# Expert stages of a two-layer macaron block: gate and up weights fetched per block into four fixed buffers and used as the stationary operand

## The chip, the cores and the metric

The kernel runs on one core of one Trainium2 chip. The metric is the device time of one execution in microseconds (us); the median of the runs is what counts.

## The reference

Four batches of 512 rows of 256 features pass through seven steps. Only the two that use `_L1_ffn_ref` are touched:

```python
    x = x + 0.5 * _L0_ffn_ref(_layernorm(x), ...)
    x = x + _L0_attn_ref(_layernorm(x), ...)
    x = x + 0.5 * _L0_ffn_ref(_layernorm(x), ...)
    x = x + 0.5 * _L1_ffn_ref(_layernorm(x), ...)     # stage m1
    x = x + _L1_attn_ref(_layernorm(x), ...)
    x = x + 0.5 * _L1_ffn_ref(_layernorm(x), ...)     # stage m2

    def _L1_ffn_ref(hidden_states, gate_weight, up_weight, down_weight, topk_idx, topk_weight):
        B, S, H, I, E, K = (4, 512, 256, 128, 32, 4)
        ...
        xs = x[tok_sorted]                    # rows ordered by expert, 4 experts per row
        g = jax.lax.ragged_dot(xs, jnp.swapaxes(gate_weight, 1, 2), group_sizes)
        u = jax.lax.ragged_dot(xs, jnp.swapaxes(up_weight, 1, 2), group_sizes)
        hmid = jax.nn.silu(g) * u
        o = jax.lax.ragged_dot(hmid, jnp.swapaxes(down_weight, 1, 2), group_sizes)
        o = o * flat_weight[perm][:, None]
        y = jnp.zeros((n, h), dtype=x.dtype).at[tok_sorted].add(o)
```

The experts are drawn anew from the inputs, so which expert a block of rows needs is known only at run time. All of it is in fp32.

## The kernel before, in words

**The whole.** `program` builds four stages that follow each other in each engine's stream: `first_layer` (the first three steps, and the routing of rows to experts), `moe_stage` with the tag m1, `latent_stage` (the second attention), `moe_stage` with the tag m2. There is no scheduler: each engine's program is written out by hand in a function of its own, and the order on an engine is the order in the code. Engines meet at semaphores (`wait_ge`, `then_inc`).

**Rows and blocks.** The 2,048 rows times 4 experts are laid out in DRAM (`rows_dram`) in blocks of 128 rows, a block having one expert. `NRUN` is 95 blocks, run in both expert stages. GpSimd scatters each normalised row to its place with an indirect DMA whose row numbers lie in `slot` (number = block times 128 plus place in the block). `block_expert` holds the expert of each block in SBUF.

**The arena.** `arena` is 96 KB per partition and, in an expert stage, holds the gate and up weights of all 32 experts (`GU`, 64 KB per partition, 512 columns per expert) and behind them the down weights (`DW`, 32 KB). In the attention stages the same bytes hold other things, so the weights are loaded in six parts of 2 MB: `early` (parts 4 and 5, which are DW), `middle` (0 and 2) and `late` (1 and 3) for m1, and three again during `latent_stage` (`reloads`: part 3, 5, 4).

**One block of an expert stage.** TensorE turns the block's rows (two transposes, L1267, into `psX`); ScalarE copies them to `xgT` (L1182); TensorE multiplies with the rows as the stationary operand and 256 columns of gate and up weights as the moving one, twice because 256 features are two partitions' worth (L1276, into `psG`, which then has rows on partitions); ScalarE takes the silu of the gate half (L1188, `sg`), VectorE multiplies it with the up half (L1214, `hm`); TensorE turns that (L1285, `psH`), VectorE copies it (L1221, `hT`), TensorE multiplies with the down weights (L1292, `psY`), ScalarE copies the result (L1194, `ys`, eight buffers), and GpSimd scatters it to `outs_dram` (the indirect DMA of L167). An fp32 product is two records in the trace, two passes over the moving operand; a transpose is one.

**The order on TensorE** is a software pipeline over blocks: in step b the transposes of block b+1, the load of block b's expert number into a register (`value_load`, L1270), the gate and up product of block b, the turn of `hm` of block b-1, the down product of block b-2. The expert number sets the address of the weights of L1276 and L1292.

**The order on SyncE's queue**: four 128 KB loads for the first four blocks, then one load of 512 KB per group of four blocks into one of two halves of `xg` (L1131), each waiting until a half is free (`turned`). Behind each of these stands, in m1, one of 16 loads of weights for the second attention (L1154) and in m2, at eight of them, a copy of a batch of `x` out to DRAM (L1146) or back in another order (L1151).

**The ends.** Before a stage TensorE waits for all weights (`experts_in`) and for the scattered rows (`placed`). After the last block, SyncE waits until all outputs have landed (`saved`), and the gathering of outputs begins.

## Time and profile before

| | us |
|---|---|
| median of 3 runs | 1455.6 (1455.46 to 1456.02) |
| profiled execution | 1455.02 |
| its span, first to last instruction | 1453.2 |
| m1, from the first transposes to the last blocks | 508 to 669 |
| m2, the same | 1256 to 1420 |
| TensorE matmuls busy | 1252.3, 86% of the span |
| VectorE, ScalarE, GpSimd busy | 950.3, 670.5, 490.6 |
| DMA moved | 151.87 MB, mean 105 GB/s |

The profile has a page and a trace. The page gives busy time per engine, the span in 40 slices, the chain of work that ended last, and the costliest groups of instructions. A group of TensorE has a busy time that counts overlapping records once and a mean duration of one record that includes the drain of the array, so records overlap and their mean times their count is more than the time they take. What a pass really takes in the stream is read from the chain of waits, or from a run of many. The trace answers for a stretch, a line, a tile or a queue.

### The profile page before, as it was taken

To read this page: it belongs to the slowest core of one execution; us is meant where nothing else is said; L and a number is where in the kernel's file an instruction comes from. 1 tells how busy PE (TensorE), PEld (TensorE's weight loads), DVE (VectorE), ACT (ScalarE), POOL (GpSimd) and SP (SyncE) were. 2 spreads that over 40 slices of the span, in tenths; PEclk is the share of its full clock that TensorE was granted. 3 is DMA by queue.
4 is the path that set the end of the run, shared out by engine and by line. 5 is a ranking of instruction groups with operands and counts; after the bars stand their busy time and mean duration, and the time that the engine had idled before them with its cause. 6 is when DMAs were issued, how large, how long until landed. Compare 5 with 4: busy or idle time off the path is not lost.

```text
span 1453.2 us, 22278 instructions
## 1 busy us (share of the span) xinstructions
PE 1252.3 (86%) x6593; PEld 818.3 (56%) x6594; DVE 950.3 (65%) x2794; ACT 670.5 (46%) x1700; POOL 490.6 (34%) x493
## 2 busy tenths in 40 slices
PE   6879888898888399998879799889889997699997
PEld 4554243343324388886645466546556655578886
DVE  6796758777778422224698878987988794133334
ACT  2205655556563055553345444554455453255550
POOL 3054040053123645552211211251143143455550
PEclk8989999999999699999998899999999999799999
DMA  8527543066313266544011000020000102355647
GB/s 288 110 31 122 183 73 58 1 120 187 135 40 146 98 232 202 193 158 170 15 44 30 20 10 1 12 105 1 2 35 24 59 30 94 127 193 179 210 140 304
DMA packets 79119, 151.87 MB, mean 105 GB/s; under 512 B 11677, under 2 KB 60254, under 8 KB 75422
## 3 DMA queue, kind: packets, MB, share of 16 engines
q1 hardware_dynamic: 63310, 108.59, 25.7%
q0 software_dynamic: 15264, 41.70, 8.0%
q8 instruction: 59, 0.97, 0.3%
q14 instruction: 54, 0.44, 0.1%
q10 hardware_dynamic: 432, 0.17, 0.0%
HBM read 85.29 MB, written 64.75 MB: 103 GB/s over the span
## 4 chain that ended last, share of the span: by engine, by line
PE 54%; DVE 28%; ACT 8%; issue 5%; DMA 3%; POOL 2%; SPq 0%; DVEq 0%; ACTq 0%; POOLq 0%
PE m_psG L1276 12%; PE m_psY L1292 6%; DVE a_t L1740 4%; DVE a_mx L924 4%; PE a_psA L1490 3%; DVE a_nb L1748 3%; PE a_psO L482 3%; ACT a_pr L1609 3%; PE m_psX L1267 3%; PE a_psU L1478 3%; PE a_psO L1514 2%; PE a_psU L457 2%; PE a_psU L1469 2%; PE a_psS L468 2%; PE a_psW L447 2%
## 5 line engine op out<-in xcount | busy, mean ns | idle before, releaser
L1609 ACT ACTIVATE a_pr<-a_psA,a_nb 128x512 f32<-128x512 f32 (+3 forms) x256 | 132.6, 524 | 229.9 <-DVE a_nb L1748 227.8
L167 POOL DMA_INDIRECT outs_dram<-m_ys,dest x190 | 182.2, 959 | 153.4 <-ACT m_ys L1194 148.2
L1214 DVE TENSOR_TENSOR m_hm<-m_psG,m_sg 128x128 f32<-128x128 f32 x190 | 55.3, 291 | 250.9 <-ACT m_sg L1188 249.8
L924 DVE TENSOR_REDUCE a_mx<-a_psU 128x1 f32<-128x512 f32 x256 | 163.3, 683 | 64.3 <-PE a_psU L457 63.1
L1276 PE MATMUL m_psG<-arena,m_xgT 128*128 x760 | 199.4, 385 | 3.6 <-ACT m_xgT L1182 3.5
L1664 POOL TENSOR_TENSOR a_q<-a_q,a_t 64x512 f32<-64x512 f32 x64 | 81.0, 1266 | 347.6 <-DVEq L1743 323.9
L167 POOL DMA_INDIRECT rows_dram<-a_xd,slot x112 | 114.1, 1019 | 157.1 <-DVE a_xd L147 72.8
L610 ACT ACTIVATE a_P<-a_psS 128x512 f32<-128x512 f32 x256 | 142.7, 597 | 51.2 <-PE a_psS L468 48.9
L1276 PEld LDWEIGHTS m_psG<-arena,m_xgT 128*128 128x128 f32 x760 | 129.5, 190 | 18.7 <-issue 7.5
L1748 DVE TENSOR_REDUCE a_nb<-a_psA 128x1 f32<-128x512 f32 (+3 forms) x256 | 113.2, 484 | 30.9 <-PE a_psA L1493 21.5
L457 PE MATMUL a_psU<-arena 96*128 96x512 bf16 x256 | 102.1, 399 | 26.2 <-DVE a_mx L924 24.8
L1292 PE MATMUL m_psY<-arena,m_hT 128*128 x380 | 113.6, 382 | 0.0
L468 PE MATMUL a_psS<-arena 108*128 108x512 bf16 x256 | 98.3, 389 | 9.6 <-ACT a_P L610 9.1
L1490 PE MATMUL a_psA<-arena,a_q 128*128 128x512 f32 (+3 forms) x256 | 91.9, 471 | 16.7 <-ACT a_pr L1609 16.0
L1758 DVE TENSOR_SCALAR a_pr<-a_pr,a_rec 128x512 f32<-128x512 f32 (+3 forms) x256 | 98.0, 404 | 6.8
L1182 ACT COPY m_xgT<-m_psX 128x256 f32<-128x256 f32 x190 | 71.8, 378 | 64.6 <-PE m_psX L1267 64.4
L1188 ACT ACTIVATE m_sg<-m_psG 128x128 f32<-128x128 f32 x190 | 52.7, 277 | 91.0 <-PE m_psG L1276 90.9
L1194 ACT COPY m_ys<-m_psY 128x256 f32<-128x256 f32 x190 | 70.7, 372 | 51.3 <-PE m_psY L1292 51.0
L1490 PE MATMUL a_psA<-a_kT,a_q 128*128 128x512 f32 (+3 forms) x256 | 87.8, 453 | 7.5 <-ACT a_pr L1609 7.3
L1598 ACT COPY a_prT<-a_psP 128x1280 f32<-128x1280 f32 x64 | 78.8, 1231 | 28.7 <-PE a_psP L1504 28.7
L1740 DVE TENSOR_TENSOR a_t<-a_psU,la_sin 32x512 f32<-32x512 f32 x128 | 87.9, 687 | 1.7
L1504 PE MATMUL a_psP<-ident,a_pr 128*128 128x128 f32 x640 | 81.8, 275 | 2.0 <-ACT a_prT L1598 2.0
(299 smaller groups left out, 2286.2 us busy)
## 6 DMA issues: line engine op xcount, KB each, us to landing
m_xg<-rows_dram SPq DMA_DIRECT2D x46, 512.0 KB, 4.2
arena<-in_mo_w SPq DMA_DIRECT2D x9, 2048.0 KB
arena<-part_dram SPq DMA_DIRECT2D x96, 128.0 KB, 5.9
arena<-outs_dram SPq DMA_DIRECT2D x20, 512.0 KB, 4.0
rows_dram<-a_P SPq DMA_DIRECT2D x6, 1024.0 KB, 11.6
part_dram<-a_part SPq DMA_DIRECT2D x16, 384.0 KB, 5.4
rows_dram<-arena SPq DMA_DIRECT2D x6, 1024.0 KB, 13.0
arena<-outs_dram SPq DMA_DIRECT2D x6, 1024.0 KB, 12.0
```

The costliest lines, as they stand in the source:

```text
L167: pool.indirect_dma_start(out=rows_dram, out_offset=bass.IndirectOffsetOnAxis(ap=slot[:, c:c + 1], axis=0), in_=row, in_offset=None).then_ ...
L457: pe.matmul(psU[n % 2][:, :], QS[0:NT, o + h * L + qt * P:o + h * L + (qt + 1) * P], KS[0:NT, o + h * L:o + (h + 1) * L], start=True, stop ...
L468: pe.matmul(psS[n % 2][:, :], KS[0:KC, o + h * L + kt * P:o + h * L + (kt + 1) * P], QS[0:KC, o + h * L:o + (h + 1) * L], start=True, stop ...
L610: act.activation(Pr[:, o:o + L], psS[c % 2][:, :], ACT.Exp).then_inc(exp_done, 1)
L924: dve.tensor_reduce(mx[g % 2][:, 4 * kt + qt:4 * kt + qt + 1], psU[n % 2][:, :], AX, ALU.max).then_inc(u_free, 1)
L1276: ins = pe.matmul(psG[b % 2][:, 0:2 * INTER], xgT[:, (b % 2) * D + k * P:(b % 2) * D + (k + 1) * P], GU[:, ds(e * (KD * 2 * INTER) + k * 2 ...
L1292: pe.matmul(psY[m % 2][:, 0:D], hT[:, (m % 2) * P:(m % 2 + 1) * P], DW[:, ds(e * D, D)], start=True, stop=True).then_inc(y_done, 1)
L1490: pe.matmul(psA[:, AT[t]:AT[t] + (t + 1) * P], qh[:, t * P:(t + 1) * P], kh[:, 0:(t + 1) * P], start=(t == BANKS[k][0]), stop=False, skip_ ...
L1609: ins = act.activation(pr[S % 2][:, AT[t]:AT[t] + (t + 1) * P], psA[:, AT[t]:AT[t] + (t + 1) * P], ACT.Exp, bias=nb[S % 2][:, t:t + 1], sc ...
L1740: ins = dve.tensor_tensor(t2[to:to + 32, o:o + L], psU[lo:lo + 32, :], la.sin[lo:lo + 32, :], ALU.mult)
L1748: ins = dve.tensor_reduce(nb[s % 2][:, t:t + 1], psA[:, AT[t]:AT[t] + (t + 1) * P], AX, ALU.max, negate=True)
L1758: ins = dve.tensor_scalar(pt, pt, rec[s % 2][:, t:t + 1], None, ALU.mult)
```

## The change

What it does:

- The rows of an expert stage are stored in another order. A new tile `place` holds (row number modulo 128) times 96 plus (row number divided by 128), so a partition's rows of successive blocks lie side by side in DRAM. VectorE makes it once, in `first_layer` (`places`, six small operations at step i = 1, p = 1 of the hand-written order), and the scatters of both stages use it. A group's load is then 128 pieces of 4 KB and not 512 of 1 KB.
- The gate and up weights no longer lie in SBUF as a whole. SyncE's queue fetches each block's 512 columns (256 KB, 128 pieces of 2 KB) from DRAM into one of four buffers at the start of the arena, `owned(b)`. It waits until the product of block b-4 is done (`gu_done`), reads `block_expert` into a register of its own, and issues the load. That is 95 times per stage, between the loads of rows and of the other weights. The first four need no wait.
- `middle`, `late` and the first of the three `reloads` are gone; DW is loaded as before.
- TensorE's gate and up product swaps its operands: the weights are stationary, the 128 rows are the moving operand. Four matmuls of 128 columns replace two of 256. The result has the inner features on partitions, so `hm` is already what the down product needs: the turn of `hm` (L1285), its copy (L1221), `psH` and `hT` go, and the down product moves up from step b-2 to b-1. TensorE has a new wait on `owned_in` before the product.
- ScalarE copies the output of block b-2 in step b where it was b-3.

The diff, cut to what carries it:

```diff
+            def places():
+                a, b, fa, fb = (counts[:, n * NC:(n + 1) * NC] for n in range(4))
+                dve.wait_ge(slots_ready, 1)
+                dve.tensor_scalar(a.bitcast(I32), slot[:, :], P - 1, None, ALU.bitwise_and)
+                link(dve.tensor_scalar(b.bitcast(I32), slot[:, :], 7, None, ALU.logical_shift_right))
+                dve.tensor_copy(fa, a.bitcast(I32))
+                link(dve.tensor_copy(fb, b.bitcast(I32)))
+                link(dve.scalar_tensor_tensor(out=fa, in0=fa, scalar=float(NBLK), in1=fb, op0=ALU.mult, op1=ALU.add))
+                dve.tensor_copy(place[:, :], fa).then_inc(places_ready, 1)
...
-                    scatter(pool, b * TPB * TOPK + n, slot, rows_dram, row, placed[b % 2])
+                    scatter(pool, b * TPB * TOPK + n, place, rows_dram, row, placed[b % 2])
...
-            for dst, src in late:
-                sp.dma_start(dst, src).then_inc(experts_in, 16)
...
-    GU, DW = weights[:, 0:NE * KD * 2 * INTER], weights[:, NE * KD * 2 * INTER:]
+    GU, DW, WIDE, NW = weights[:, 0:NE * KD * 2 * INTER], weights[:, NE * KD * 2 * INTER:], KD * 2 * INTER, len(owned_in)
+    owned = lambda b: GU[:, b % NW * WIDE:(b % NW + 1) * WIDE]
...
-                sp.dma_start(xg[:, o:o + GRP * D].rearrange("p (j d) -> p j d", d=D),
-                             rows_dram[g * GRP * P:(g + 1) * GRP * P, :].rearrange("(j p) d -> p j d", p=P)
-                             ).then_inc(block_in[g % NX], 16)
-
+                sp.dma_start(xg[:, o:o + GRP * D], rows[:, g * GRP * D:(g + 1) * GRP * D]).then_inc(block_in[g % NX], 16)
+
+            def load_expert(b):
+                if b >= NW:
+                    sp.wait_ge(gu_done, b - NW + 1)
+                e = sp.value_load(block_expert[0:1, b:b + 1], min_val=0, max_val=NE - 1)
+                sp.dma_start(owned(b), experts[:, ds(e * WIDE, WIDE)]).then_inc(owned_in[b % NW], 16)
+
+            for b in range(NW):
+                load_expert(b)
...
-            for g in range(NX, NGRP):
+            for n in range(NW, NRUN):
+                load_expert(n)
+                g = (n - 1) // GRP + 1
+                if (n - 1) % GRP or not NX <= g < NGRP:
+                    continue
                 load(g)
...
-            for b in range(NRUN + 3):
+            for b in range(NRUN + 2):
...
-                m = b - 3
+                m = b - 2
                 if 0 <= m:
                     act.wait_ge(y_done, m + 1)
...
-                        dve.wait_ge(h_turned, b - 1)
+                        dve.wait_ge(y_done, b - 1)
...
-                    dve.tensor_copy(hT[:, (m % 2) * P:(m % 2 + 1) * P], psH[m % 2][:, 0:P]).then_inc(hT_ready, 1)
...
-                    for k in range(KD):
-                        ins = pe.matmul(psG[b % 2][:, 0:2 * INTER], xgT[:, (b % 2) * D + k * P:(b % 2) * D + (k + 1) * P],
-                                        GU[:, ds(e * (KD * 2 * INTER) + k * 2 * INTER, 2 * INTER)],
-                                        start=(k == 0), stop=(k == KD - 1))
+                    pe.wait_ge(owned_in[b % NW], 16 * (owned_times[b % NW] + b // NW + 1))
+                    for half in range(2):
+                        for k in range(KD):
+                            w = k * 2 * INTER + half * INTER
+                            ins = pe.matmul(psG[b % 2][:, half * P:(half + 1) * P], owned(b)[:, w:w + INTER],
+                                            xgT[:, (b % 2) * D + k * P:(b % 2) * D + (k + 1) * P],
+                                            start=(k == 0), stop=(k == KD - 1), skip_group_check=True)
                     ins.then_inc(gu_done, 1)
...
-                    pe.transpose(psH[m % 2][:, 0:P], hm[:, (m % 2) * P:(m % 2 + 1) * P], ident[:, :]).then_inc(h_turned, 1)
-                m = b - 2
...
-                    pe.matmul(psY[m % 2][:, 0:D], hT[:, (m % 2) * P:(m % 2 + 1) * P], DW[:, ds(e * D, D)],
+                    pe.matmul(psY[m % 2][:, 0:D], hm[:, (m % 2) * P:(m % 2 + 1) * P], DW[:, ds(e * D, D)],
```

How the rows stand on TensorE in the middle of m1, for one block, before (an ISA row sets a register; TENSOR_LOAD is the `value_load`; in brackets what is waited for):

```order
L1270 TENSOR_LOAD block_expert
L1270 ISA x2
L1276 ISA [waits m1_hm_ready,m1_xT_ready]
L1276 MATMUL m_psG<-arena,m_xgT 128x256
L1276 ISA
L1276 MATMUL m_psG<-arena,m_xgT 128x256
L1285 MATMUL m_psH<-ident,m_hm 128x128 [waits m1_hT_ready,m1_hm_ready]
L1292 ISA [waits m1_y_copied,m1_hT_ready]
L1292 MATMUL m_psY<-arena,m_hT 128x256
L1267 MATMUL m_psX<-ident,m_xg 128x128 [waits m1_xT_ready]
L1267 MATMUL m_psX<-ident,m_xg 128x128
```

And in the changed kernel, by its own line numbers:

```order
L1284 TENSOR_LOAD block_expert
L1284 ISA x2
L1292 MATMUL m_psG<-m_xgT,arena 128x128 [waits owned_in2,m1_hm_ready,m1_xT_ready]
L1292 MATMUL m_psG<-m_xgT,arena 128x128 x3
L1302 ISA [waits m1_y_copied,m1_hm_ready]
L1302 MATMUL m_psY<-arena,m_hm 128x256
L1281 MATMUL m_psX<-ident,m_xg 128x128 [waits m1_xT_ready,m1_block_in1]
L1281 MATMUL m_psX<-ident,m_xg 128x128
```

The register loads of L1276 are gone, the product is four matmuls with one more semaphore ahead of it, the turn is gone, and the down product waits for `hm` itself.

On SyncE's queue in m1, twelve blocks before the change (three groups of four):

```order
L1131 DMA m_xg<-rows_dram 128x4x256 [waits m1_turned]
L1154 DMA la_raw<-in_la_qup 128x1536
L1131 DMA m_xg<-rows_dram 128x4x256 [waits m1_turned]
L1154 DMA la_raw<-in_la_kup 128x1024
L1131 DMA m_xg<-rows_dram 128x4x256 [waits m1_turned]
L1154 DMA la_raw<-in_la_vup 128x1024
```

And the beginning of one group in the changed kernel (the last four rows stand there four times before the next group's first row; the `la_` tiles are those of the second attention's weights):

```order
L1141 DMA m_xg<-rows_dram 128x1024 [waits m1_turned]
L1174 DMA la_raw<-in_la_kup 128x1024
L1146 TENSOR_LOAD block_expert [waits m1_gu_done]
L1146 ISA x2
L1147 ISA
L1147 DMA arena<-in_mo_w 128x512
```

Between two loads of rows the queue now waits four times for TensorE, reads SBUF four times and issues four loads.

## Rows read from the trace of the kernel before

**Rows 1.** Page, costliest groups: busy us, mean ns | idle before, what ended it.

```profile
L1276 PE MATMUL m_psG<-arena,m_xgT 128*128 x760 | 199.4, 385 | 3.6 <-ACT m_xgT L1182 3.5
```

**Rows 2.** Windows m1, m2: length, busy us per engine, clock, DMA share, GB/s.

```profile
508.00:669.00 161.00, 159.74 (x864) 132.32 (x864) 46.76 (x190) 89.58 (x288) 89.99 (x94) 0.99 0.56 189
1256.00:1420.00 164.00, 160.80 (x872) 133.45 (x872) 54.43 (x231) 89.36 (x286) 90.11 (x94) 1.00 0.52 176
```

**Rows 3.** Chain of waits, one block of m1: start us, us, what.

```profile
585.61 0.22 PE m_psX L1267 x2
585.83 0.86 PE m_psG L1276 x4
586.70 0.11 PE m_psH L1285
586.81 0.43 PE m_psY L1292 x2
```

**Rows 4.** Line L1276 in m1, then m2: ns min/median/max, first to last start.

```profile
L1276 PE MATMUL m_psG<-arena,m_xgT x380: 378/380/581, 509.4 to 665.3; 128*128 x190
...
L1276 PE MATMUL m_psG<-arena,m_xgT x380: 378/380/479, 1257.6 to 1416.1; 128*128 x190
```

**Rows 5.** Timeline, 28 fp32 matmuls of 128 columns, after m2's blocks.

```profile
1418.54 6.41 PE L162 MATMUL m_psX<-ident 128*128 128x128 f32 x56
```

**Rows 6.** Timeline of m1 around one block: start, us, engine, operation, idle before.

```profile
586.73 0.28 ACT L1188 ACTIVATE m_sg<-m_psG 128x128 f32<-128x128 f32 x1 [0.44 <-PE m_psG L1276]
...
587.04 0.29 DVE L1214 TENSOR_TENSOR m_hm<-m_psG,m_sg 128x128 f32<-128x128 f32 x1 [1.14 <-ACT m_sg L1188]
```

**Rows 7.** Timeline, the last outputs of m2 leaving through GpSimd.

```profile
1417.74 0.96 POOL L167 DMA_INDIRECT outs_dram<-m_ys,dest  x1 [0.62 <-ACT m_ys L1194]
...
1420.27 0.96 POOL L167 DMA_INDIRECT outs_dram<-m_ys,dest  x1 [0.30 <-issue]
```

**Rows 8.** Line L1270 on TensorE's sequencer in m1, then in m2.

```profile
L1270 PEldq TENSOR_LOAD <-block_expert x95: 295/432/762, 508.4 to 663.6; - x95
...
L1270 PEldq TENSOR_LOAD <-block_expert x95: 296/407/1477, 1255.8 to 1414.3; - x95
```

**Rows 9.** Line L1270 on TensorE's sequencer, then the timeline of m1 beside it.

```profile
L1270 PEldq TENSOR_LOAD <-block_expert x1: 644/644/644, 587.8 to 587.8; - x1
...
587.29 1.06 PE L1276 MATMUL m_psG<-arena,m_xgT 128*128 x4
...
589.03 1.12 PE L1276 MATMUL m_psG<-arena,m_xgT 128*128 x4
```

**Rows 10.** Line L1270, then timeline: the worst stretch of m2.

```profile
L1270 PEldq TENSOR_LOAD <-block_expert x1: 1403/1403/1403, 1276.0 to 1276.0; - x1
...
1278.01 0.48 PE L1276 MATMUL m_psG<-arena,m_xgT 128*128 x1 [0.58 <-ACT m_xgT L1182]
```

**Rows 11.** SyncE's queue in m1: issues of one group.

```profile
585.86 0.36 SPq L1131 DMA_DIRECT2D m_xg<-rows_dram  x1
586.26 0.56 SPq L1154 DMA_DIRECT2D la_cos<-in_la_cos  x1
```

**Rows 12.** DMA issues, median us to landing last; then DMA from 1428 to 1436.

```profile
m_xg<-rows_dram SPq DMA_DIRECT2D x46, 512.0 KB, 4.2
...
DMA packets 467, 3.43 MB, mean 429 GB/s; under 512 B 48, under 2 KB 48, under 8 KB 48
```

**Rows 13.** DMA from 595.4 to 597: a load of 2 KB pieces beside a scatter.

```profile
DMA packets 356, 0.60 MB, mean 377 GB/s; under 512 B 46, under 2 KB 179, under 8 KB 355
q1 hardware_dynamic: 291, 0.40, 68.0%
q0 software_dynamic: 64, 0.20, 30.9%
```

**Rows 14.** Tile `slot`: where GpSimd makes it, and a small operation on it.

```profile
L954 POOL CAST slot<-arena x1: 237/237/237, 96.4 to 96.4; 128x64 int32<-128x64 f32 x1
L695 DVE TENSOR_SCALAR a_qf<-slot x1: 185/185/185, 418.8 to 418.8; 128x64 int32<-128x64 int32 x1
```

More of the change, by code:

```diff
@@ L172, with first_layer @@
 GROUPS = B * H // HPG
-def first_layer(nc, block, sem_of, stored, r, ident, ring, wt, wmain, wlora, iota, bias_qk, bias_v, bias_o, part_dram, slot, rows_dram,
-                placed, early, middle, late, experts_in, weight, block_expert, dest, dest_in, spare, first_loads,
+def first_layer(nc, block, sem_of, stored, r, ident, ring, wt, wmain, wlora, iota, bias_qk, bias_v, bias_o, part_dram, slot, place, rows_dram,
+                placed, early, experts_in, weight, block_expert, dest, dest_in, spare, first_loads,
                 route_loads, row_loads, rest_loads):
@@ L825, in side @@
                     absorb(4, 8)
+                if i == 1 and p == 1:
+                    places()
                 if i == B and p == 0:
@@ L977, in rows @@
                 if b == 0 and lo == 0:
+                    pool.wait_ge(places_ready, 1)
                     for n in range(2):
@@ L1208, in _ @@
         def _(dve):
-            for b in range(NRUN + 1):
+            for b in range(NRUN):
                 if b < NRUN:
@@ L1254, in _ @@
             expert = {}
-            for b in range(-1, NRUN + 2):
+            for b in range(-1, NRUN + 1):
                 m = b + 1
@@ L1270, in _ @@
                     expert[b] = pe.value_load(block_expert[0:1, b:b + 1], min_val=0, max_val=NE - 1)
-                    e = expert[b]
                     pe.wait_ge(xT_ready, b + 1)
@@ L1681, in _ @@
                 sp.dma_start(pk[t % NP], picked_rows(out_dram, t)).then_inc(picked[t % NP], 16)
-            (first, first_src), (low, low_src), (high, high_src) = reloads
-            sp.wait_ge(added, TILES * TOPK)
-            sp.dma_start(first, first_src).then_inc(experts_in, 16)
+            (low, low_src), (high, high_src) = reloads
             made(sp, ("o", B - 2, TPB - 1))
@@ L1921, in program @@
         ident, iota = sb("ident", [P, P]), sb("iota", [P, P + 1 + TOPK + TILES])
-        slot, dest = sb("slot", [P, NC], I32), sb("dest", [P, NBLK], I32)
+        slot, place, dest = sb("slot", [P, NC], I32), sb("place", [P, NC], I32), sb("dest", [P, NBLK], I32)
         block_expert, weight = sb("block_expert", [1, NBLK], I32), sb("weight", [P, NC])
@@ L1929, in program @@
         picked = [sem(f"picked{i}") for i in range(10)]
+        owned_in = [sem(f"owned_in{i}") for i in range(4)]
+        owned_times = {"m1": [0] * 4, "m2": [len(range(i, NRUN, 4)) for i in range(4)]}
         half = arena.shape[1] // 6
         load = lambda c: (arena[:, c * half:(c + 1) * half], a["mo_w"][:, c * half:(c + 1) * half])
-        early, middle, late = [load(4), load(5)], [load(0), load(2)], [load(1), load(3)]
+        early = [load(4), load(5)]
         tiles_of = lambda lo, hi: (r.x[:, lo * TPB * D:hi * TPB * D].rearrange("p (t d) -> p t d", d=D),
@@ L1941, in program @@
             first_layer(
-                nc, block, sem, stored[0], r, ident, arena, aw, wmain, wlora, iota, bqk, bv, bo[:, :], part_dram, slot, rows_dram, placed[0],
-                early, middle, late, experts_in, weight, block_expert, dest, dest_in, a["c_spare"], [
+                nc, block, sem, stored[0], r, ident, arena, aw, wmain, wlora, iota, bqk, bv, bo[:, :], part_dram, slot, place, rows_dram, placed[0],
+                early, experts_in, weight, block_expert, dest, dest_in, a["c_spare"], [
                     tiles_of(0, 1), (wmain[:, :], a["ff_main"]), (wlora[64:65, :], a["ff_bias"]),
@@ L1957, in program @@
                 la.prepare(c2, nc, a, latent_in, latent_kept)
-                moe("m1", placed[0], stored[0], 6, la, None)
-            latent_stage(nc, block, sem, stored[1], r, ident, la, slot, rows_dram, placed[1], arena[:, 4 * half:],
-                         arena[:, 3 * half:4 * half], weight, outs_dram, [load(3)] + early, experts_in, picked[0:4])
+                moe("m1", placed[0], stored[0], 2, la, None)
+            latent_stage(nc, block, sem, stored[1], r, ident, la, place, rows_dram, placed[1], arena[:, 4 * half:],
+                         arena[:, 3 * half:4 * half], weight, outs_dram, early, experts_in, picked[0:4])
         with ExitStack() as c:
             by_four = c.enter_context(nc.sbuf_tensor("by_four", [P, NC], F32))
-            moe("m2", placed[1], stored[1], 9, None, (out, written, by_four, a["mo_by_four"], x_dram, picked, [TILES // 4] * 4 + [0] * 6))
+            moe("m2", placed[1], stored[1], 4, None, (out, written, by_four, a["mo_by_four"], x_dram, picked, [TILES // 4] * 4 + [0] * 6))
 def kernel(**inputs):
```

39 lines of the change are left out of this document (14 added, 25 removed).

## The prediction

> **What bounds the kernel now.** I read the page first. The product with the gate and up weights is TensorE's costliest group, and the idle time in front of all its 760 records is 3.6 us [rows 1]. The windows then give the stages: TensorE is busy for 159.7 of 161 us in m1 and 160.8 of 164 in m2, at the full clock, while VectorE and ScalarE have half their time or more free [rows 2]. So inside the two expert stages TensorE is the bound, and the chain of waits runs on TensorE alone there. The chain gives each piece the time it takes in the stream: transposes 0.22, gate and up 0.86 in four passes, the turn 0.11, the down product 0.43, in sum 1.62 us per block [rows 3]. The real step is a little longer: 94 steps from 509.4 to about 664.6 (the last product's first pass, 0.65 ahead of its last one) make 1.65 us in m1, and 94 steps from 1257.6 to 1415.4 make 1.68 in m2 [rows 4]. A further view tells why. TensorE's sequencer reads the block's expert number from SBUF, which takes 432 ns in the median but up to 762 ns in m1 and 1477 ns in m2 [rows 8]. Two products in a row start at 587.29 and 589.03, 1.74 apart, with one read of 0.64 between them [rows 9]; so everything else that this sequencer does for a block takes up to 1.10 us. Over many blocks with a long read I take 1.06, which is an estimate from rows of this kind. Reads under about 0.56 us are hidden behind a step of 1.62, longer ones are not. The worst, 1403 ns, left TensorE idle for 0.58 us before the next product [rows 10]. DMA is at 0.56 and 0.52 of its time, 189 and 176 GB/s [rows 2].
>
> **The passes.** Four passes of 256 columns (0.86) become eight of 128. Such passes stand in the trace with a weight load each, as here: 56 records in 6.41 us, the last with its drain of 0.27, so 6.14 / 55 = 0.112 us each [rows 5]. Eight are 0.89. The price cannot be much lower, since the work of two passes of 128 columns is that of one of 256 (0.215), and the row would have to be wrong for it to be higher. The turn (0.11) goes. The step is then 0.22 + 0.89 + 0.43 = 1.54, which is 0.08 less than 1.62: 190 blocks give -15 us (from -13 to -17 by the rounding of the rows).
>
> The down product moves one step earlier, so `hm` of block b-1 must be ready when the product of block b ends. After the last pass of a product at 585.83 + 0.86 = 586.69 [rows 3], silu ends at 587.01 and the multiplication at 587.33 [rows 6], 0.63 us later. Between the two lie the down product, two transposes and 0.89 of the next product. Nothing waits. VectorE's copy and ScalarE's order cost nothing either: both engines have half their time free [rows 2].
>
> **The ends of the stages.** Without the turn, its copy, and one step of the pipeline, the last down product can start about 0.8 us earlier, and the last two outputs no longer come together. In the profile GpSimd starts the last scatters at 1417.74 and 1420.27, one after the other at its own pace of 1.27 [rows 7]. In the new order the last but one leaves in its turn and the last can start near 1418.8: -1.5 us per stage, -3 in all (0 to -3.5).
>
> **TensorE's sequencer.** It loses two register settings and the turn, gains four matmul issues and a wait. I leave its 1.06 us as it is. A read longer than 1.54 - 1.06 = 0.48 us then shows, where it was 0.56. In m1 the excess over the chain's 1.62 is 0.03 per step, or 3 us with the opening; the lower threshold and a busier DMA about double it. I take +5 us for both stages. Below it ends at 0 (reads do not get slower). Above, if each block lost 0.1, it would be +19; the rows nearest to that are single blocks beside loads.
>
> **SyncE's queue.** For a block it now waits, reads the number, sets registers and issues. On TensorE the read that begins at 587.8 and takes 0.64 is followed by the product at 589.03, 0.59 after its end [rows 9]; with a median read that is 0.43 + 0.59, or 1.0. The issue of a load takes 0.36 to 0.56 [rows 11]. That is 1.4 to 1.6 us; to it comes a quarter of the issue of the rows (0.10) and in m1 a quarter of the other weights' (0.14). So 1.5 to 1.7 without, 1.64 to 1.84 with those, against a step of 1.54. TensorE's register work is the fuller one of the two, with register settings for a product that a load does not have, and the plain form of a load stands at the low end of the issues, so I take the range's lower edge less a tenth: 1.43 without the others and 1.55 with. That is about the step. This term costs nothing in the forecast, and it is the first rival.
>
> The Trainium skill, DMA: Bandwidth & Descriptors, section Latency and other measured facts, gives such a register load a floor of about 600 ns. The rows disagree, with 295 at the least and 432 in the median, and the measurement decides; by the page's figure, an estimate for the queue would be 1.6 us or more per block, and it would be the bound.
>
> **The loads of weights.** A load is issued some 0.9 us after the product of block b-4 ends, and it is needed when the product of b starts, 3 steps and 0.65 us after that end, or 5.3. Loads of 512 KB land in 4.2 us [rows 12], and one of 256 KB cannot need more. From the issue, 0.9 behind the end, that is 5.1 at the worst: alone, a load is in time. What can be late is the sum. A block now moves 256 KB of weights, 128 of rows, 128 of outputs. With 2 KB pieces, 1 KB pieces and a scatter in flight, DMA reached 377 GB/s with all its time used [rows 13]. Four blocks are 2.10 MB, 5.6 us of a group's 6.2: it fits, at nine tenths of DMA's time. Where a further 512 KB stands in the group, it is 2.62 MB or 6.95 us, 0.75 too long; 768 KB make it 1.45 too long. In m1 seven groups have 512 KB (or nearly) and one has 768: 6.7 us. In m2 eight groups have 512 KB, with a group between them that has 0.6 to spare: some 2 us. What the lead absorbs once is small beside it. I take +8. The bounds: 0 if the rate in a heavy group reaches 2.62 / 6.2 = 423 GB/s, which one copy of large pieces did (429) [rows 12]. At 345 GB/s, a tenth under the 377, a plain group takes 6.1 us and fits, and a heavy one is 1.4 too long: 16 of them make +22.
>
> The rows' own load gets cheaper by the change (4 KB pieces for 1 KB), which is in the 377. In front of the stages nothing is gained by the loads removed: TensorE waited there for the scattered rows, and the weights had landed.
>
> **`places`.** `slot` is made at 96.4, and six operations of 0.185 [rows 14] stand at i = 1, far behind it, in a stretch where VectorE is often the bound: +1.1 if all of it shows, 0 if none. I take +0.6. The scatters by `place` move the same 1 KB rows: 0.
>
> **The sum**, against the profiled execution's 1455.0: -15 - 3 + 5 + 8 + 0.6 = -4.4, so 1450.6 us. That execution lies 0.6 below the median of the three runs, less than the terms' own error. Differences under 0.2%, or 2.9 us, are about what a measurement of this kernel can't tell from no change.
>
> **Rivals.**
> 1. SyncE's queue becomes the bound. For it: the range above reaches 1.84, and a step from the wait to the issue is serial, as nothing else can fill it. Against it: TensorE's reads have a median of 0.43. It decides from 1.54 per block on. At 1.70 in the mean, 190 times 0.15 is 28 us, in place of the +5 and +8: 1455 - 15 - 3 + 0.6 + 28 = 1466. Slower. Chance 25%.
> 2. DMA keeps up: the heavy groups are carried by the lead, and the 8 us fall away, 1442.6. For it: the 429 GB/s of the large copy [rows 12]. Chance 16%.
> 3. Loads of 256 KB run far below the rate of large ones through the whole of both stages. At 240 GB/s a load takes 1.09 us, with outputs 0.35 and rows 0.35 that is 1.79 per block, 0.25 over the step, 47 us in place of 8: 1485. The row against it is the 377 of a stretch in which one such load was in flight [rows 13]. Chance 9%.
>
> The Trainium skill, DMA: Bandwidth & Descriptors, section Bandwidth, measured 138 GB/s for 64 KB and 341 for 1 MB and says to batch to 1 MiB; the third rival is that rule's. Its figures are for one load at a time, and no run here shows that for 256 KB.
>
> **How the numbers follow.** The forecast as it stands has 50%, with a range of its own from 1445 to 1456; nearly two thirds of it are faster by over 2.9 us, and the rest is within. Rival 2 is faster. Rivals 1 and 3 are slower. Faster: 0.33 + 0.16 = 0.49. Same: 0.17. Slower: 0.34. The range reaches from 1441, which takes in most of rival 2, to 1472, which takes in most of rival 1; rival 3 and the tops of the others stay outside.
>
> **What the profile of the changed kernel would show.** The passes: eight records of the gate and up product in 0.89 us in the chain, and a step of 1.54 where nothing is late. The queue: if it is the bound, SyncE shows no waits for `gu_done` and TensorE's idle time before the product is ended by a DMA in every block. The loads: idle time ended by DMA only in m1's first half and at the copies of `x` in m2. The sequencer: idle "issue" before the product, and reads above 0.43 in the median. The ends: GpSimd's last scatter 1.5 us after its last but one or less. I would be wrong if passes with changing weights took more than 0.112 us, or if the queue's work per block came out over 1.54.

## The result, and the profile after

The changed kernel takes 1506.4 us in the median of four runs (1491.1 to 1507.3), against 1455.8 for the kernel before in the same comparison: 1.031 times, with a 95% interval from 1.028 to 1.034. It is slower by 51 us. The forecast was 1450.6, with a range that ended at 1472.

The profiled execution took 1505.6 us, with a span of 1503.8. First the page: two of its costliest groups and two of its DMA issues.

```profile
L1292 PE MATMUL m_psG<-m_xgT,arena 128*128 128x128 f32 x1520 | 212.9, 285 | 52.0 <-DMA arena<-in_mo_w 48.0
L1302 PE MATMUL m_psY<-arena,m_hm 128*128 x380 | 118.1, 394 | 0.7 <-DVE m_hm L1234 0.7
...
arena<-in_mo_w SPq DMA_DIRECT2D x190, 256.0 KB, 4.4
m_xg<-rows_dram SPq DMA_DIRECT2D x46, 512.0 KB, 5.8
```

The idle time before the product was 3.6 us [rows 1] and is 52.0, and a load of weights ended 48.0 of it. The windows of m1 and m2, with the columns of [rows 2]:

```profile
511.00:691.00 180.00, 156.25 (x1136) 141.44 (x1135) 27.69 (x95) 88.83 (x285) 89.16 (x93) 0.97 0.88 299
1278.00:1470.00 192.00, 162.99 (x1149) 147.17 (x1148) 35.58 (x136) 89.77 (x286) 90.14 (x94) 0.94 0.82 274
```

TensorE, busy for 159.7 of 161 us before, now has 24 and 29 us free, and DMA's share has gone from 0.56 and 0.52 to 0.88 and 0.82. The product's line gives the steps (first and last start, as in [rows 4]):

```profile
L1292 PE MATMUL m_psG<-m_xgT,arena x760: 272/275/553, 511.3 to 689.8; 128*128 128x128 f32 x190
...
L1292 PE MATMUL m_psG<-m_xgT,arena x760: 273/275/551, 1279.1 to 1467.6; 128*128 128x128 f32 x190
```

Less the seven passes from a product's first to its last (0.78), 94 steps take 177.7 us in m1, 1.89 each, and 187.7 in m2, 2.00 each. They were 155.2 and 157.8. So the stages lost 22.5 and 29.9 us, 52.4 together. The first product of m1 starts 1.9 us later than before, and what lies between the stages and behind them is 3.9 shorter; that makes 50.4 of the 50.6 by which the spans differ.

Where nothing is late, the chain of waits shows the forecast step (m1, start us, us, what; the piece of 0.43 is the down product, as in [rows 3]):

```profile
566.22 0.43 PE m_psY L1302 x2
566.66 0.22 PE m_psX L1281 x2
566.88 0.89 PE m_psG L1292 x8
567.77 0.43 PE m_psY L1302 x2
```

Eight passes in 0.89, and a step of 1.55. Between such stretches the chain leaves TensorE:

```profile
617.22 0.91 PE m_psG L1292 x8
...
618.14 0.28 SPq L1146
...
618.87 0.34 SPq L1147
619.21 0.04 issue
619.25 0.43 SPq L1141
619.69 0.04 issue
619.73 0.44 SPq L1174
620.17 0.06 issue
620.22 0.27 SPq L1146
...
620.92 6.48 DMA arena<-in_mo_w
```

SyncE reads the expert number (L1146) and issues a load of weights (L1147) from 618.14 to 619.21: 1.07 us for a block. Then it issues the rows (512 KB) and one of the second attention's tables (64 KB), and after them the next load of weights, which takes 6.48 us. A stall of this kind can cost more than its own length. The timeline just before this stretch shows the first work after an earlier stall of 3.11 us, and the windows show the granted clock around two such stalls:

```profile
612.59 0.42 PE L1292 MATMUL m_psG<-m_xgT,arena 128*128 128x128 f32 x1
612.80 1.06 PE L1302 MATMUL m_psY<-arena,m_hm 128*128 x2
```

```profile
520.00:530.00 10.00, 6.83 (x40) 6.05 (x39) 0.87 (x3) 2.88 (x10) 3.18 (x4) 0.83 0.87 333
610.00:620.00 10.00, 9.04 (x59) 8.39 (x60) 1.17 (x4) 3.97 (x13) 3.66 (x4) 0.83 0.75 258
```

A pass record of 0.275 is 0.42 here and the down product 1.06 instead of 0.60: for a part of these 10 us TensorE ran at 1.2 GHz after it had stood idle. Not every stall has this behind it, and its length alone does not decide. Two more stalls of m1, with the windows behind them:

```profile
540.56 1.13 PE L1292 MATMUL m_psG<-m_xgT,arena 128*128 128x128 f32 x8 [2.23 <-DMA arena<-in_mo_w]
...
578.82 1.24 PE L1292 MATMUL m_psG<-m_xgT,arena 128*128 128x128 f32 x8 [1.98 <-DMA arena<-in_mo_w]
```

```profile
540.00:546.00 6.00, 5.44 (x43) 5.17 (x44) 0.88 (x3) 2.77 (x9) 2.02 (x3) 1.00 1.02 398
580.00:583.00 3.00, 3.00 (x14) 2.71 (x13) 0.29 (x1) 1.02 (x3) 0.96 (x1) 0.50 1.02 316
```

After 2.23 us of idleness the clock stayed full, after 1.98 it was at 1.2 GHz.

### The profile page after: what moved, and what is told of

Its sections match the earlier page's. It is cut to its first block, busy times and chain, and to the rows that moved or that the text cites. A ratio compares the mean times of both kernels' runs of the same rounds, so it can differ in the third digit from the quotient of the medians.

```text
span 1503.8 us, 23626 instructions
## 1 busy us (share of the span) xinstructions
PE 1254.9 (83%) x7164; PEld 844.5 (56%) x7164; DVE 914.3 (61%) x2610; ACT 670.2 (45%) x1700; POOL 490.6 (33%) x493
## 4 chain that ended last, share of the span: by engine, by line
PE 41%; DVE 28%; DMA 13%; ACT 8%; issue 6%; SPq 3%; POOL 2%; DVEq 0%; ACTq 0%; POOLq 0%
DMA arena<-in_mo_w 10%; PE m_psG L1292 7%; DVE a_t L1748 4%; DVE a_mx L936 4%; DVE a_nb L1756 3%; PE a_psA L1500 3%; PE a_psO L482 3%; ACT a_pr L1619 3%; PE a_psU L1488 3%; PE a_psU L457 2%; PE a_psU L1479 2%; PE a_psW L421 2%; PE a_psO L1524 2%; PE m_psY L1302 2%; PE a_psS L468 2%
## 5 line engine op out<-in xcount | busy, mean ns | idle before, releaser
L1292 PE MATMUL m_psG<-m_xgT,arena 128*128 128x128 f32 x1520 | 212.9, 285 | 52.0 <-DMA arena<-in_mo_w 48.0
L1292 PEld LDWEIGHTS m_psG<-m_xgT,arena 128*128 128x128 f32 x1520 | 193.1, 199 | 61.7 <-issue 45.8
L167 POOL DMA_INDIRECT rows_dram<-a_xd,place x112 | 114.2, 1019 | 157.9 <-DVE a_xd L147 72.6
L1302 PE MATMUL m_psY<-arena,m_hm 128*128 x380 | 118.1, 394 | 0.7 <-DVE m_hm L1234 0.7
L1500 PE MATMUL a_psA<-arena,a_q 128*128 128x512 f32 (+3 forms) x256 | 88.0, 454 | 16.5 <-ACT a_pr L1619 16.0
## 6 DMA issues: line engine op xcount, KB each, us to landing
rows_dram<-arena SPq DMA_DIRECT2D x6, 1024.0 KB, 14.3
```

What stands on the lines that cost most here:

```text
L167: pool.indirect_dma_start(out=rows_dram, out_offset=bass.IndirectOffsetOnAxis(ap=slot[:, c:c + 1], axis=0), in_=row, in_offset=None).then_ ...
L1292: ins = pe.matmul(psG[b % 2][:, half * P:(half + 1) * P], owned(b)[:, w:w + INTER], xgT[:, (b % 2) * D + k * P:(b % 2) * D + (k + 1) * P], ...
L1302: pe.matmul(psY[m % 2][:, 0:D], hm[:, (m % 2) * P:(m % 2 + 1) * P], DW[:, ds(e * D, D)], start=True, stop=True).then_inc(y_done, 1)
L1500: pe.matmul(psA[:, AT[t]:AT[t] + (t + 1) * P], qh[:, t * P:(t + 1) * P], kh[:, 0:(t + 1) * P], start=(t == BANKS[k][0]), stop=False, skip_ ...
```

## The experiments

All of them keep the loads, the product and the rest of the changed kernel unless a diff says otherwise. The kernels of one group ran on one chip, beside the kernel before (1459.7, 1458.3, 1460.2, 1460.8 and 1462.2 us in the five groups). The chips turned out to matter, and the last part of this section is on that; until then what is compared stood on one chip.

**Group 2: fewer bytes, more buffers, no loads.** The first is the changed kernel as it is.

> The changed kernel itself, run beside the three kernels below. In the profiles of e1_small and e1_sixteen TensorE's signals of a finished product came up to 1.6 us late at 19 to 22 places of a stage, which the profiles of the kernel before and of the changed kernel do not show at all (at most 0.02 us). Expected where that is absent: 1506, m1 in 178 us and m2 in 188 from first to last product. Where it is present: up to 1520.

Measured: 1505.9 us, 1.035 (1.029 to 1.041).

```diff
-                sp.dma_start(owned(b), experts[:, ds(e * WIDE, WIDE)]).then_inc(owned_in[b % NW], 16)
+                n = WIDE if b < NW else 16
+                sp.dma_start(owned(b)[:, 0:n], experts[:, ds(e * WIDE, n)]).then_inc(owned_in[b % NW], 16)
```

> As e1_small: 8 KB in place of 256 KB for each weight load after the first four of a stage (most blocks multiplied with weights of an earlier load). If the rest of e1_small's excess (16 and 18 us in the two stages) came from the late signals: 1431 to 1445 here if they are absent, and then the bytes are the whole cause. If it comes from SyncE's queue: 1460 to 1480 again, with an idle time of TensorE in each group of four blocks.

Measured: 1455.3 us, 0.998 (0.996 to 1.001). Taking 97% of the weights' bytes away brings 50.6 us, with SyncE's waits, reads and issues untouched. So its queue is not the bound. But 1455 is not 1431 to 1445: stalls are left. In m1 7.5 of the 8.5 us over 94 steps of 1.546 stand at loads of weights right behind a load of rows. The chain of waits shows one, 8 KB issued behind rows and another 512 KB:

```profile
538.04 5.79 DMA arena<-in_mo_w
543.83 0.14 issue
543.96 1.13 PE m_psG L1293 x8
```

The next has all its bytes, but eight buffers:

```diff
-    GU, DW, WIDE, NW = weights[:, 0:NE * KD * 2 * INTER], weights[:, NE * KD * 2 * INTER:], KD * 2 * INTER, len(owned_in)
+    GU, DW, WIDE, NW = weights[:, 0:NE * KD * 2 * INTER], weights[:, NE * KD * 2 * INTER:], KD * 2 * INTER, 8
+    SHARE = NW // len(owned_in)
...
-                sp.dma_start(owned(b), experts[:, ds(e * WIDE, WIDE)]).then_inc(owned_in[b % NW], 16)
+                sp.dma_start(owned(b), experts[:, ds(e * WIDE, WIDE)]).then_inc(owned_in[b // SHARE % 4], 16)
```

> The changed kernel with 8 weight buffers in place of 4, one semaphore for each pair. If the delay is that of a load behind a megabyte in the queue (rows 512 KB and other weights 512 KB), four more blocks of lead (6.2 us) carry it: within 5 us of what sixteen buffers give. If the rate over many groups is short, eight buffers run dry and it stands between four and sixteen: 1480 to 1495.

Measured: 1446.1 us, 0.993 (0.990 to 0.995). The part of the edit that is not shown keeps the loads of rows at their place in time and lets TensorE wait for the weights in pairs. It is 59.8 us faster than the changed kernel with the same bytes through the same queue, and 9 faster than with 8 KB loads and four buffers. The windows from 540 to 580 of e2_after, then of e2_eight:

```profile
540.00:580.00 40.00, 35.56 (x239) 32.60 (x238) 5.83 (x20) 18.47 (x59) 18.21 (x19) 0.88 0.90 307
```

```profile
540.00:580.00 40.00, 39.12 (x294) 35.22 (x293) 7.00 (x24) 22.61 (x73) 23.55 (x25) 1.00 1.05 382
```

DMA can move what the step of 1.55 asks for: 382 GB/s. With four buffers it moved 307. A load does not land sooner for it. For the changed kernel the line of the loads gives, in m1, how long TensorE waited for them (us, times), and minimum, median and maximum from issue to landing,

```profile
  PE m_psG L1292: 22.0, 16
...
DMA to landing us min/median/max: 2.5/4.4/7.1
```

and for e2_eight, where TensorE hardly waits, the loads are no quicker:

```profile
DMA to landing us min/median/max: 2.6/5.0/5.7
```

With four buffers a load is asked for when the product of block b-4 has ended. SyncE's read and register work take 0.8 us, and the product of block b is due 5.3 us after that end. So 4.4 to 4.5 us are left, and landings take up to 7.1. Most loads still come in time. With each landing of m1 in the trace set beside the first pass of its product, half of the 91 loads that had to wait for a buffer have 0.97 us or more to spare (the stalls in between lengthen their lead), and 20 are late (the product starts within 0.2 us of the landing). Of the 23 that stand right behind a load of rows in the queue 16 are late, of the other 68 four. The steps of those 23 blocks hold 23.8 of the 32.4 us that m1 takes over 94 steps of 1.546; in m2 it is 25.1 of 42.4. While TensorE stands the next loads are not asked for either, so DMA does not get ahead. Eight buffers add 6.2 us to the 4.5; in m1 of e2_eight the blocks whose load stands behind rows hold 0.1 of the 6.8 us over 94 such steps.

**Weights resident, copied inside SBUF.** The same product and the same order, with no load per block: the six parts of weights are loaded as before the change, and VectorE fills one of three fixed buffers.

```diff
+            def hold(b):
+                if b >= 3:
+                    dve.wait_ge(gu_done, b - 2)
+                e = dve.value_load(block_expert[0:1, b:b + 1], min_val=0, max_val=NE - 1)
+                dve.tensor_copy(held(b), GU[:, ds(e * WIDE, WIDE)]).then_inc(w_ready, 1)
```

> Weights resident as before the change, so no load per block; VectorE copies a block's 512 columns from the arena into one of three fixed buffers (address from the expert number that it reads), and the product, the order of the rows and the pipeline are those of the changed kernel. If the step of 1.546 us is right and only the loads broke it: -0.08 to -0.10 us per block and the ends, 1435 to 1443. VectorE was busy 0.29 of 1.62 us per block and gets 0.4 to 0.6 us more. If TensorE's swapped product has a cost of its own that the loads hid, 1450 or more.

Measured: 1435.8 us, 0.986 (0.982 to 0.989), 22.6 us under the kernel before. The product in m1 and m2, and VectorE's copy:

```profile
L1297 PE MATMUL m_psG<-m_xgT,m_wb x760: 273/275/347, 511.2 to 657.4; 128*128 128x128 f32 x190
...
L1297 PE MATMUL m_psG<-m_xgT,m_wb x760: 273/275/377, 1248.7 to 1397.5; 128*128 128x128 f32 x190
```

```profile
L1226 DVE COPY m_wb<-arena x92: 426/492/499, 513.7 to 654.4; 128x512 f32 x92
```

94 steps take 145.4 us, 1.547 each, and 148.0. The copy of 0.49 us and the 0.29 of the multiplication are half of VectorE's step. So the swapped product is worth what it was said to be, and the loads with four buffers cost the rest: 1505.9 - 1435.8 = 70 us.

**Group 1: the order alone, and the same questions on another chip.**

> The kernel before with one part of the change alone: expert rows in DRAM ordered by partition, then block (place, its six operations, the row loads in 4 KB pieces). Weights resident as before. If the order costs only its six operations: 1455.6 + 0 to 1 us. If scattered rows land slower at their new places, or the six operations delay more than themselves, it shows here: the changed kernel's first product of m1 starts 1.9 us later than before (511.3 against 509.4), so up to +2 (or +4 if m2 pays it too).

Measured: 1459.3 us, 0.999 (0.997 to 1.001), with the diff's parts on `place` and the row loads in the kernel before. The order of the rows and its six operations cost nothing that can be measured.

> The changed kernel, but after the first four loads of a stage each weight load moves only 16 of its 512 columns (8 KB, 128 pieces of 64 B, in place of 256 KB). SyncE still waits, reads the expert number, and issues 95 loads per stage; TensorE still waits for each. Left out: most blocks are multiplied with weights that an earlier load left. Theory A (the bytes are too many for DMA): the idle time before the product that a DMA ended goes. m1's 94 steps took 178 us (1.89 each) and m2's 188 (2.00), where 1.546 would make 145; that is 75 us in all, so 1506 - 75 = about 1431, up to 1440. Theory B (SyncE's queue: wait, read, issue in series): the queue does what it did, so the time stays at 1495 or more.

Measured: 1475.1 us, 1.009 (1.005 to 1.012).

> The changed kernel, but after the first four loads of a stage each weight load moves 256 of its 512 columns (128 KB, 128 pieces of 1 KB). Left out: half the product's weights are those of an earlier load. Theory A: a plain group of four blocks needs 1.57 MB, at the 306 GB/s that m1 as a whole reached 5.1 us of the 6.2 it has; a group with a further 512 KB needs 2.1 MB or 6.9 us, 0.7 too long. So stalls are small and only in heavy groups: 1436 to 1455. Theory B: 1495 or more.

Measured: 1473.6 us, 1.009 (1.006 to 1.012); the edit is that of e2_small with 256 for 16.

> The changed kernel with 16 weight buffers in place of 4, one semaphore for each four of them; the loads run up to 15 blocks ahead and carry the same bytes. Theory A, the rate is short all the time: the two stages move about 55 MB each; DMA was busy 0.88 and 0.82 of them, so with no gaps they take at least 158 and 157 us in place of 178 and 188: 1450 to 1470. Theory A2, only heavy groups are short, and four buffers are too few to carry them: 1431 to 1445. If the depth changes nothing (1495 to 1510), the gaps in DMA's time come from SyncE's queue.

Measured: 1473.0 us, 1.008 (1.005 to 1.010). The edit is that of e2_eight with 16 buffers, four to a semaphore.

Three ways to relieve the loads end within about 2 us of each other, and none at 1431 to 1445. On this chip something else holds them, which e2_small and e2_eight on theirs do not show (below). What the group does settle: SyncE's queue would have left e1_small at 1495 or more.

**Groups 4 and 5: is it the place in the queue?** e2_small's load of 8 KB that took 5.79 us, and the place of the late loads in m1, say yes. So the rows, the second attention's weights and the copies of `x` were given to ScalarE's queue, which issues them after its copy into `xgT`:

```diff
             for n in range(NW, NRUN):
                 load_expert(n)
-                load(g)
...
                     act.copy(xgT[:, (b % 2) * D:(b % 2 + 1) * D], psX[b % 2][:, 0:D]).then_inc(xT_ready, 1)
+                g = (b + 1) // GRP + 1
+                if (b + 1) % GRP == 0 and NX <= g < NGRP:
+                    load(q, g)
```

> The changed kernel with four buffers and all its bytes, but the loads of rows, the second attention's weights and the copies of x leave through ScalarE's DMA queue, so that no weight load stands behind them in SyncE's. Theory F (first in, first out: a weight load behind up to a megabyte lands in 5.6 us in the median and up to 7.2, and four buffers bear about 5.1): the weight loads land sooner and the time falls by a third of the 50 us or more, to 1450 to 1485. Theory R (the DMA engines' rate is short whatever the order): 1495 to 1515, with the same idle time before the product. ScalarE issues 0.45 to 0.9 us per group more, which its half free time hides.

Measured: 1514.6 us, 1.040 (1.036 to 1.044), in the range of theory R.

> e2_small (8 KB weight loads, most blocks with weights of an earlier load) and the two queues of e4_two_queues together. e2_small left 14 and 18 us over 94 steps of 1.546, in stalls of 0.9 to 3.3 us, each behind a load of rows and another of 512 KB. Theory F: these go, 1432 to 1442. If they were SyncE's own work (reads of the expert number and issues), at most half of its issues leave it and 1445 to 1455 stay.

Measured: 1461.3 us, 1.001 (0.999 to 1.004), the two edits together.

> The changed kernel beside the three below. If this chip shows TensorE's signals late (as in e1_small, e1_sixteen and the three e4 kernels) it gives what that costs the changed kernel: between 1500 and 1525. Without them 1506.

Measured: 1508.0 us, 1.034 (1.029 to 1.039).

> As e4_two_queues (rows, other weights and copies of x through ScalarE's queue), now beside the changed kernel on one chip. Theory F (a weight load is late because of what stands ahead of it in its queue): at least 15 us less than e5_after. Theory W (what is late is any load while DMA is nearly full: with four buffers a load is asked for only 4.4 us before it is needed, and the 16 DMA engines share themselves between the queues): within 10 us of e5_after.

Measured: 1525.8 us, 1.045 (1.042 to 1.049), 18 us more than e5_after beside it. The queue's order alone as the cause falls: with all its bytes, a second queue makes it worse. In m1 37 steps are over 1.546 by more than 0.2 us, where e5_after has 26. The bound for theory W, within 10 us, is missed as well, on the slow side. That fits a DMA that shares itself between two queues, so that the megabyte no longer stands only in front of some loads but beside all of them; no run shows that sharing by itself. With 8 KB loads the second queue seems to help (1461 against e1_small's 1475), but these two did not stand on one chip in one group, and it decides nothing.

**The order of the rows at the shorter step.**

> e3_copy without the new order of the rows (scatter by slot, row loads in 512 pieces of 1 KB as before the change). e1_order showed no difference for the order alone, so 1435.8 again within 3 us. If 1 KB pieces at the shorter step make the row loads late, 1440 or more and idle time of TensorE before the transposes.

Measured: 1453.1 us, 0.994 (0.992 to 0.996).

> As e3_copy (resident weights, VectorE copies a block's columns into a fixed buffer), as the anchor for the next kernel: 1436 where signals are prompt, up to 1455 where they are late.

Measured: 1467.6 us, 1.005 (1.003 to 1.007).

> As e4_copy_slot (the same without the new order of the rows). If its 1453 came from the late signals: within 3 us of e5_copy. If the order of the rows is worth something at the shorter step: 10 to 17 us more than e5_copy.

Measured: 1464.8 us, 1.002 (1.000 to 1.004). Side by side the order is worth nothing here either, within 3 us. But e5_copy is e3_copy, and it took 32 us more.

**The chips.** Before and changed kernel hardly differ between the groups (1458 to 1462, 1506 and 1508). Kernels in which TensorE could run nearly without a stall do: e3_copy took 1436, and 1468 and 1469 (e5_copy, e6_copy). The timelines, of e3_copy, then of e5_copy, show it at ScalarE (in brackets the idle time before):

```profile
554.36 0.28 ACT L1201 ACTIVATE m_sg<-m_psG 128x128 f32<-128x128 f32 x1 [0.46 <-PE m_psG L1297]
...
555.90 0.28 ACT L1201 ACTIVATE m_sg<-m_psG 128x128 f32<-128x128 f32 x1 [0.47 <-PE m_psG L1297]
```

```profile
564.22 1.06 PE L1297 MATMUL m_psG<-m_xgT,m_wb 128*128 128x128 f32 x8
...
566.77 0.28 ACT L1201 ACTIVATE m_sg<-m_psG 128x128 f32<-128x128 f32 x1 [1.16 <-PE m_psG L1297]
...
567.53 0.69 PE L1307 MATMUL m_psY<-arena,m_hm 128*128 x2 [0.70 <-DVE m_hm L1238]
```

A product whose records end at 565.28 is followed by its silu at 566.77, 1.5 us late, and TensorE then waits 0.70 us for `hm`. In e3_copy the silu starts 0.04 us after the end at all but one block of each stage. In e5_copy it is over 0.3 us late at 30 blocks of m1, and this is where the time goes: of 15.0 us over 94 steps of 1.546, 13.9 stand in 18 long steps, and in each of them the down product starts within 0.2 us of an `hm` whose silu was late. The counts go with the chips: once in a stage in e2_eight (1446.1), 27 and 25 times in e6_eight (1467.7); 22 and 11 times in e4_copy_slot (1453.1), 30 and 28 in e5_copy_slot (1464.8). The last group tried to cover this with slack: rows turned two blocks ahead, down product two blocks behind.

```diff
-            for b in range(-1, NRUN + 1):
-                m = b + 1
+            for b in range(-2, NRUN + 2):
+                m = b + 2
```

> As e3_copy and e5_copy, which gave 1436 on one chip and 1468 on another; the anchor for the next kernel. 1436 if ScalarE's silu starts 0.04 us after the end of every product, 1450 to 1470 if it starts over 0.3 us late at 20 or more places of a stage.

Measured: 1468.8 us, 1.004 (1.002 to 1.005).

> e3_copy with one more step between a result and its use: TensorE turns the rows two blocks ahead (three buffers of xgT) and multiplies with the down weights two blocks behind (three of hm). If late signals of TensorE are what e5_copy lost its 30 us to, the slack of one more step (1.55 us) covers delays of up to 1.5 us and it stands at 1437 to 1445 on any chip; where signals are prompt it costs the one step more per stage, 1 to 3 us over e6_copy. If the loss has another cause, it stands where e6_copy does.

Measured: 1469.7 us, 1.005 (1.003 to 1.007). The time did not move, but this does not clear the late signals. In its m1 the silu is over 0.3 us late at 60 blocks, by up to 1.85 us, and a step of 2.0 us returns about every 5.2 us, every third block:

```profile
557.85 0.28 ACT L1201 ACTIVATE m_sg<-m_psG 128x128 f32<-128x128 f32 x1 [2.25 <-PE m_psG L1297]
...
558.16 0.29 DVE L1238 TENSOR_TENSOR m_hm<-m_psG,m_sg 128x128 f32<-128x128 f32 x1 [1.75 <-ACT m_sg L1201]
...
558.55 1.13 PE L1297 MATMUL m_psG<-m_xgT,m_wb 128*128 128x128 f32 x8 [0.33 <-issue]
```

The product of block b still waits for `hm` of block b-2, because `psG` has two buffers in this kernel too. All 28 long steps of m1, 13.3 of its 14.3 us over 1.546, start 0.10 us after that `hm` ends. So the edit gave slack at two waits and the lateness came through at a third.

> As e2_eight, which gave 1446 where signals were prompt. The same here if they are; 1465 to 1480 if they are late, since sixteen buffers gave 1473 then.

Measured: 1467.7 us, 1.005 (1.003 to 1.007), as in the second half of its expectation.

Why a product's result reaches ScalarE late on these chips was not found, and stays open; the ends of TensorE's records are modelled, so it can also be that the products themselves end later than the trace has it. What it leaves standing: on the chip of group 2 eight buffers or a copy inside SBUF turn the change into a gain of 12 or 23 us; on the chips of groups 5 and 6 both end some 6 us above the kernel before, and still 40 below the changed one; the copy in the old order of rows was 7 us below the kernel before on the chip of group 4. Neither can be called a version that beats both.

## The prediction, step by step

- **The bound before, and the passes (-15): right.** Neither of the signs of being wrong that the prediction names came. The step is 1.546 to 1.547 where nothing is late (forecast 1.54), seen in the changed kernel and over all of m1 in e3_copy. Against before, e3_copy's 94 steps are 9.8 us shorter in each stage.
- **The ends of the stages (-3): right in size.** After the last pass of the last product in m2 the kernel before took 1453.2 - 1416.1 = 37.1 us to its end, the changed one 1503.8 - 1467.6 = 36.2. From m1's last to m2's first product it was 592.3 us and is 589.3. That is 3.9 in all, the part between the stages with its own scatter from run to run (591.3 in e3_copy, 588.1 in e2_eight). GpSimd's last scatter of m2 starts 1.26 us after its last but one, as forecast.
- **TensorE's sequencer (+5): wrong in sign.** It was to be 5 us worse with a busier DMA. The reads became shorter (302 ns in the median of m1, 503 at most, where [rows 8] have 432 and 762), and in e3_copy's m1 no more than 0.1 us is left over the step. Over both stages 8.4 us stood above the chain's 1.62 before and 2.8 stand above 1.546 in e3_copy: -5.6 us.
- **SyncE's queue (0 in the forecast, rival 1): right not to take it.** A load costs it 1.07 us, where the prediction had 1.4 to 1.6; with a quarter of the rows' issue that is 1.19, not the 1.43 taken, and e2_small, which has that whole queue, stands 50 us lower.
- **The loads of weights (+8, 0 to +22): this step failed.** The lead was worked out rightly: 5.3 us from one end to the other. The landing was the median of the row loads before the change (4.2 us for 512 KB, with DMA at 0.56 of its time), and "alone, a load is in time" closed the matter; what is late was then counted in bytes per group against a rate, and stalls were expected in groups with a further 512 KB only. In fact 0.8 us and a median landing of 4.4 leave next to nothing of the 5.3, and right behind the rows, with outputs and other weights under way, landings reach 7.1: 16 of 23 such loads of m1 are late, through the whole stage, and the idle time is not confined to m1's first half and the copies of `x`. The rate was good: 377 GB/s was forecast, and e2_eight reached 382. With four buffers it is the lead that holds the rate at 307, and not the other way round. The term measured about 70 us on the chip of e3_copy; with eight buffers it is 10, near the 8 that the sum had.
- **Stalls and the clock: not in the sum at all.** After some of the stalls TensorE ran at 1.2 GHz for a while (three in m1, of 3.17, 1.98 and 3.11 us; not after 2.23). The mean granted clock was 0.97 over 180 us of m1 and 0.94 over 192 of m2, against 0.99 and 1.00 before, so an estimate of its price is up to 5 and 11 us. The busy time of 156.3 us in m1 is 9 over 95 steps of 1.546; the slower passes are in these 9, with what else keeps it busy longer not told apart.
- **`places` (+0.6): within what can be measured.** e1_order shows no difference. The first product of m1 starts at 511.3, 1.9 us later than before, but three profiles of one kernel start it at 511.2, 509.9 and 514.5 (e3_copy, e5_copy, e6_copy), so this is scatter.
- **The rivals.** The third, at 1485, came nearest in time (47 us in place of the 8 alone make 1490; 1485 also drops the 5 of the sequencer), and DMA's rate did stay low through both stages (299 and 274 GB/s, where it had 240). But its reason, a size that DMA serves badly, was not the cause: with the same 256 KB loads e2_eight moved 382. The Trainium skill, DMA: Bandwidth & Descriptors, section Bandwidth, has 138 GB/s for 64 KB and 341 for 1 MB and advises to batch to 1 MiB or more. No run here measures a single load of 256 KB; e2_eight shows another remedy than size, more loads at once. The second rival (1442.6) is what e2_eight came near to.
- **The range** ended at 1472. With its highest end of +22 the term of the loads makes 1465, so no value that it was given could reach 1506. Stalls behind two thirds of the loads of rows were in none of the cases.

## What to carry to other kernels

For a load that is asked for when a buffer comes free, compare the lead (buffers times step, less the work before the issue) with the landing time beside everything else that is under way, and take for that the longest landings that the trace shows, not a median from a kernel with a quieter DMA. Look first at the load that is issued right behind the largest other ones. If lead and landing are close, the buffers hold the rate down before the bytes do: here eight buffers for four took 60 us off and a second queue added 18. Bytes per group against a rate is the second check, not the first.

## What the runs showed of the hardware

- The time of TensorE's register load from SBUF goes with the form of the product and not with DMA: 432 ns in the median with DMA at 0.56, 302 in the changed kernel at 0.88, 306 in e3_copy (new product, resident weights), 398 in e1_order (old product). The first two rows of the sequencer's line in m1 of the changed kernel:

```profile
L1284 PEldq TENSOR_LOAD <-block_expert x95: 295/302/503, 510.3 to 688.1; - x95
L1284 PEldq FUSED_REGOPS  x95: 146/146/165, 510.9 to 688.4; - x95
```

- A load of 8 KB landed 5.79 us after its issue, behind a megabyte in the same queue; the whole 256 KB took 2.5 at best.
- A DMA share of 0.90 was not yet its limit: it went with 307 GB/s, and eight buffers brought 1.05 and 382, for the same mix of pieces. Over 540 to 600 us a packet of 2 KB took 102 ns in the mean in e2_after and 90 in e2_eight.
- One kernel (e3_copy) took 1436 us on one chip and 1468 on others, while the kernel before took 1458 to 1462. With it went how often ScalarE saw a product over 0.3 us late in m1: once, and 30 and 32 times. A comparison of kernels that run TensorE without a gap needs all of them on one chip.
